# Four triangle layers on one core: centre and gate products as four 64x64 corners, whole squares in two layers, spread transposes ahead of the gate product

## The reference

```python
xn = _layernorm(x, ln1_w, ln1_b)                 # layers 0, 1, 2; layer 3 has none
left  = xn @ Wl.T * m * sigmoid(xn @ Wlg.T)      # mask m in layers 0, 1 and 3
right = xn @ Wr.T * m * sigmoid(xn @ Wrg.T)
out_gate = sigmoid(xn @ Wog.T)
out = einsum('bikd,bjkd->bijd', left, right)     # 64 planes of 192x192 products
out = _layernorm(out, ln2_w, ln2_b) * out_gate
return out @ Wout.T
```

## Time and profile before

| | before |
|---|---|
| median of 3 runs | 1425.36 us |
| the profiled execution's own time | 1427.8 us |
| its span, first to last instruction | 1425.6 us |
| TensorE matmul busy | 1231.4 us (86%) |
| VectorE busy | 983.5 us (69%) |
| ScalarE busy | 920.8 us (65%) |
| GpSimd busy | 525.5 us (37%) |
| mean granted TensorE clock | 0.972 |

### The profile page before, as it was taken

One profiled execution on the slowest core, in us unless ns is written; L12 is line 12 of the kernel. 1 busy time (PEld: TensorE's weight loads), 2 busy tenths in 40 slices (PEclk: granted clock), 3 DMA queues, 4 the chain that ended last, 5 costly groups with the idle time before them and its releaser, 6 DMA issues. The chain is left out here.

```text
span 1425.6 us, 39778 instructions
## 1 busy us (share of the span) xinstructions
PE 1231.4 (86%) x11486; PEld 686.5 (48%) x11486; DVE 983.5 (69%) x2692; ACT 920.8 (65%) x1849; POOL 525.5 (37%) x490
## 2 busy tenths in 40 slices
PE   0799998789799998999982999999888788899897
PEld 0455555434344544674331555567544344467443
DVE  6577776368779999226991888842299899931587
ACT  0577775399677777227992888842499677722676
POOL 0355553045355655003551666620155200000365
PEclk9999999999889999999995999999999999999999
DMA  8011111578623332797758555549799544469898
GB/s 296 23 51 50 50 50 64 140 230 263 202 90 105 105 110 84 211 297 217 204 158 326 156 170 176 185 142 298 251 288 282 183 156 155 149 186 313 263 315 267
DMA packets 222432, 258.73 MB, mean 181 GB/s; under 512 B 54177, under 2 KB 209057, under 8 KB 222369
## 3 DMA queue, kind: packets, MB, share of 16 engines
q1 hardware_dynamic: 193920, 232.75, 52.1%
q10 hardware_dynamic: 28448, 25.17, 5.4%
HBM read 139.89 MB, written 117.96 MB: 181 GB/s over the span
## 5 line engine op out<-in xcount | busy, mean ns | idle before, releaser
L1036 DVE SCALAR_TENSOR_TENSOR lr<-ps,mask,act_out 128x128 f32 (+5 forms) x1152 | 278.8, 310 | 51.1 <-ACT act_out L785 42.9
L1195 POOL TENSOR_TENSOR rstd<-ve,half_col 128x6 f32<-128x6 f32 x144 | 190.4, 1323 | 232.0 <-DVE ve L1003 196.5
L1240 POOL TENSOR_TENSOR new_ring<-val,lr 128x384 f32<-128x384 f32 x96 | 104.0, 1084 | 372.1 <-issue 297.8
L569 PE MATMUL ps<-w_parts,val 64*128 64x256 bf16 (+1 forms) x1728 | 199.7, 310 | 18.4 <-DVE lr L1036 17.7
L785 ACT ACTIVATE act_out<-ps 128x384 f32<-128x384 f32 x384 | 176.1, 483 | 50.5 <-PE ps L579 34.3
L1228 POOL TENSOR_TENSOR val<-act_out,gate_ring 128x384 f32<-128x384 f32 x96 | 99.8, 1040 | 224.8 <-ACT act_out L855 189.5
L679 PE MATMUL ps<-in_ring,k 128*128 128x384 f32 x288 | 124.4, 517 | 26.2 <-DMA in_ring<-t_scratch 23.0
L838 ACT ACTIVATE sq<-ps 128x384 f32<-128x384 f32 x192 | 105.7, 551 | 54.0 <-PE ps L679 52.0
L1087 DVE COPY cen<-ps 128x384 f32<-128x384 f32 x48 | 26.8, 558 | 159.1 <-PE ps L637 159.1
L637 PE MATMUL ps<-lr 64*128 64x192 f32 (+3 forms) x896 | 125.8, 331 | 9.8 <-DVE lr L1036 5.2
L761 ACT ACTIVATE cen<-ps,gn 128x384 f32<-128x384 f32 x144 | 83.8, 582 | 77.1 <-PE ps L524 73.8
(11 more groups left out here) (108 smaller groups left out, 2290.0 us busy)
## 6 DMA issues: line engine op xcount, KB each, us to landing
gate_scratch<-gate_ring SPq DMA_DIRECT2D x192, 192.0 KB, 2.2
gate_ring<-gate_scratch SPq DMA_DIRECT2D x96, 384.0 KB, 3.9
lr<-x_scratch SPq DMA_DIRECT2D x72, 384.0 KB, 4.9
in_ring<-t_scratch SPq DMA_DIRECT2D x72, 384.0 KB, 3.9
x_scratch<-new_ring SPq DMA_DIRECT2D x48, 384.0 KB, 3.4
in_ring<-x_scratch SPq DMA_DIRECT2D x96, 192.0 KB, 2.4
lr<-x SPq DMA_DIRECT2D x6, 1536.0 KB, 15.5
t_scratch<-cen SPq DMA_DIRECT2D x96, 96.0 KB, 4.0
```

The source lines that it names most:

```text
L569: mm = nc.tensor.matmul(banks[h][:, :, 0:P], moving(x, s)[half(h), N * r:N * r + P], proj_weights(w, h)[:, 0:2 * P], start=start, stop=sto ...
L1036: ins = nc.vector.scalar_tensor_tensor(out5[:, h, lo // 2:hi // 2, :, m], ps[:, 4 + 2 * r + h, lo:hi].rearrange("p (a e) -> p a e", e=2), ...
L1195: nc.gpsimd.tensor_tensor(rstd[:, s % 2, :], ve[:, s % 2, :], half_col[:, :], ALU.pow)\
```

## The change

The centre product and the gate product become four products of 64x64 corners of the block-diagonal weights each (`corners`), with 192 columns, which use the four quarters of the array. They swap the layout on the way: the partitions' half becomes the tile's row, and the bank (0 or 1) the picture's half; the gate product swaps it back. Both lie in banks 0 and 1, the centre in columns 0 to 191, the gate in 192 to 383, so that the centre product of tile n+4 now waits for the gate's sigmoid of tile n, and the gate product for `cen` of the tile in flight. Centre products have one place in place of two. The variance moves to bank 3. In layers 1 and 2 it is made of the whole float32 squares with `k_sel`, three products in place of six, and `square_low` is left out there. ScalarE squares `cen` out of SBUF in place of the PSUM result. TensorE's steps of these layers are written out with no loop.

```diff
+                def corners(first, weights, x, start, stop):
+                    for q in range(2):
+                        for e in range(2):
+                            mm = nc.tensor.matmul(ps[C * e:C * e + C, q, first:first + N], weights[half(q), half(q)],
+                                                  x[half(q), N * e:N * e + N], start=start, stop=stop,
+                                                  skip_group_check=True)
+                    return mm
...
-                    slot_free(pe, a_sq, base + n - 1)
-                    slot_free(pe, a_ve, base + n - 1)
-                    nc.tensor.matmul(ps[:, s % 2, 0:TILE], w_centre[:, :], in_ring[:, s, :] if l else x_all[:, n, :],
-                                     start=True, stop=True).then_inc(a_z, 1)
+                    slot_free(pe, a_cen, base + n)
+                    if gated:
+                        pe.wait_ge(a_gate, base + n - RING + 1)
+                    corners(0, w_centre, in_ring[:, s, :] if l else x_all[:, n, :], True, True).then_inc(a_z, 1)
...
+                    slot_free(pe, a_ve, base + n)
+                    if WHOLE_VAR[l]:
+                        pe.wait_ge(a_sq, base + n + 1)
+                        for j in range(CHUNKS):
+                            mm = nc.tensor.matmul(ps[:, 3, 2 * j:2 * j + 2], sq[:, s % 2, P * j:P * j + P], k_sel,
+                                                  start=True, stop=True)
...
+                    if ln:
+                        if centred:
+                            pe.wait_ge(a_cen, base + n + RING)
+                        for w, x in passes:
+                            mm = corners(N, gate_weights(w), moving(x, s), (w, x) == passes[0], (w, x) == passes[-1])
...
                 def step(n, i, s, ahead):
-                    gate(n, s)
                     if ln and ahead >= 1:
                         spread(n + 1, (s + 1) % RING)
+                    gate(n, s, ahead >= 3)
                     project(n, s, 0)
+                    if ln and ahead >= 4:
+                        centre(n + 4, i + 1, s, True)
                     project(n, s, 1)
-                    if ln and ahead >= 4:
-                        centre(n + 4, i + 1, s)
...
-                over_tiles(pe, step)
+                if ln:
+                    for n in range(TILES):
+                        step(n, n // RING, n % RING, TILES - 1 - n)
...
                     sigmoids(n, s, 0)
+                    if ln and ahead >= 4:
+                        centred(n + 4, s)
                     sigmoids(n, s, 1)
                     if ln and ahead >= 4:
-                        centred(n + 4, s)
+                        squared(n + 4, s)
...
-                    if ln and ahead >= 3:
+                    if halved and ahead >= 3:
                         square_low(n + 3, (s + 3) % RING)
```

More of the change, by code:

```diff
@@ L58 @@
 LATE = 14
+WHOLE_VAR = (False, True, True, False)
+LOWS = tuple(sum(1 for m in range(l) if not WHOLE_VAR[m]) for l in range(LAYERS))
 T_SCALE = (1.0, 1.0, 1.0 / N, 1.0)
@@ L514, in proj_weights, with centre @@
                     return w_parts[half(h), part, :] if IN_PARTS[l] else w_whole[half(h), :]
-                def centre(n, i, s):
+                def corners(first, weights, x, start, stop):
[5 more added lines that the diff above has]
+                    return mm
+                def centre(n, i, s, gated):
                     if l == 2:
@@ L542, in spread, with gate @@
                     mm.then_inc(a_bc, 1)
-                def gate(n, s):
+                def gate(n, s, centred):
                     if IN_PARTS[l]:
@@ L807, in phase_a @@
                 if ln:
-                    centred(0, 0)
-                    centred(1, 1)
-                    centred(2, 2)
-                    centred(3, 3)
+                    for n in range(RING):
+                        centred(n, n)
+                        squared(n, n)
                     high(0, 0)
@@ L989, in phase_a @@
                 ln = HAS_LN[l]
+                halved = ln and not WHOLE_VAR[l]
                 out5 = lr_view(l).rearrange("p a e (h r) -> p h a e r", h=2)
@@ L1032, in glu @@
                     if HAS_MASK[l]:
-                        for h in range(2):
+                        for g in range(2):
+                            h, row = (r, ROWS * n + g) if ln else (g, m)
                             for t, (lo, hi) in enumerate(((0, P), (P, COLS))):
                                 ins = nc.vector.scalar_tensor_tensor(
-                                    out5[:, h, lo // 2:hi // 2, :, m],
-                                    ps[:, 4 + 2 * r + h, lo:hi].rearrange("p (a e) -> p a e", e=2),
-                                    mask4[:, t, h, bass.ds(m, 1)],
-                                    sig[:, h, lo:hi].rearrange("p (a e) -> p a e", e=2), ALU.mult, ALU.mult)
+                                    out5[:, h, lo // 2:hi // 2, :, row],
+                                    ps[:, 4 + 2 * r + g, lo:hi].rearrange("p (a e) -> p a e", e=2),
+                                    mask4[:, t, h, bass.ds(row, 1)],
+                                    sig[:, g, lo:hi].rearrange("p (a e) -> p a e", e=2), ALU.mult, ALU.mult)
                         ins.then_inc(a_free, 1)
@@ L1066, in phase_a @@
                     normalise(0, 0)
+                if halved:
                     square_low(2, 2)
```

43 lines of the change are left out of this document (26 added, 17 removed).

## The result

The changed kernel takes 1447.08 us (median of 4 runs, 1440.95 to 1451.63) against 1424.13 for the kernel before on the same chip: ratio 1.0155, 95% interval 1.0109 to 1.0202. It is slower by 1.6%; the forecast was 1424 with a range to 1438. The profiled execution took 1447.88, its span is 1445.6, TensorE's mean granted clock 0.967.

A forecast was written before the change was run, and what follows sets the result against it. TensorE was taken to bound layer 0 narrowly, VectorE's ring layer 1, TensorE with waits for `low` layer 2. Terms +3.5, 0, -4.2 and -1 (phase starts) sum to -1.7 us, giving 1424 us, range 1410 to 1438.

The forecast's parts named there:

- TensorE bounds it, but by little: Layer 0 before the change: TensorE's work sets the tile, 3.91 us, 3.95 with loop turns.
- the second ring: Layer 0's cycle of projection, sigmoid, `glu`, projection, put at 3.72 us, only 0.23 shorter than TensorE's work.
- the sum of 3.67: Layer 0: the pieces of the projection, sigmoid and `glu` cycle without the centre product, added up and checked against measured 3.72.
- Layer 0's 4.03: Forecast tile time in layer 0 with the centre product inside the cycle, against 3.95 before: +3.5 us over 44 tiles.
- The unrolled loop gives nothing: its 0.15 a turn lies in TensorE's new wait: Layer 0: writing out TensorE's loop saves no time, since the 0.15 us a turn falls where TensorE waits anyway.
- Layer 1, 0 us,: VectorE's ring stays at 3.64 us a tile, with ScalarE's second sigmoid fitting by 0.05; bounds -2 and +5.
- Layer 2, 3.30 a tile and -4.2 us,: Layer 2's tile falls from 3.395 to 3.30 us, -4.2 us over 44 tiles; bounds -11.5 and +9.
- The wait of the centre for the gate's sigmoid: Layer 2: `centre(n+4)` waits about 0.11 us a tile for the gate's sigmoid of n, bringing 3.13 to 3.24.
- TensorE's own work: Layer 2: TensorE's work without waits, 3.15 + 0.52 variance - 0.39 centre - 0.15 gate, is 3.13 us a tile.
- Some 0.06 for what is left of L1202 and `low` meeting: Layer 2: a chosen 0.06 us a tile for GpSimd's L1202 and VectorE's `low` still delaying each other.
- The slower rival: Layers 1 and 2: whole-square passes cost more than 0.11 us, deciding from about 0.13; total 1438 to 1446, chance 0.15.
- The clock: Layer 0: TensorE's waits might lower its granted clock, making the tile 5 us and the kernel 50 slower; chance 0.02.

The follow-up runs named there:

- e1: Changed kernel with the centre product and ScalarE's `cen` moved back behind the second projection and sigmoid: 1434.94 us, ratio 1.0046 to the kernel before.
- e4: Kernel before with only TensorE's loop over the tiles written out in layers 0 to 2: 1435.89 us, ratio 1.0048.
- e8: Kernel before with only VectorE's loop over the tiles written out in layers 0 and 1: 1419.90 us, ratio 0.9954.
- e13: Changed kernel with only VectorE's loop written out in layers 0 and 1: 1434.22 us, ratio 1.0043 to the kernel before.
- e7: Changed kernel with e1's and e5's edits and VectorE's loop written out in layers 0 and 1: 1413.71 us, ratio 0.9918 to the kernel before.
- e5: Changed kernel with SyncE's `keep` store issued ahead of the gathers in layer 2: 1445.74 us, ratio 1.0119 to the kernel before.
- e11: Kernel before with only the spread transposes of tile n+1 moved ahead of the gate product of n: 1419.32 us, ratio 0.9960.
- e3: e5 with the gate product of n again ahead of the spread transposes of n+1: 1437.72 us, ratio 1.0076 to the kernel before.

## Why the prediction was wrong

- **"TensorE bounds it, but by little" and the second ring** held in kind. TensorE idles for `glu` as forecast, and the centre in the ring costs 0.33, forecast 0.36. That the sum of 3.67 met the measured 3.72 was partly luck. The earlier trace rows lie in the last four tiles, which are written out behind the loop; `glu` starts 0.53 behind the first sigmoid there, while the sum's 0.65 is the loop's (0.65 in the step of the earlier trace rows too). ScalarE's and VectorE's timelines of the kernel before beside the earlier trace rows:

```profile
239.47 0.49 ACT L785 ACTIVATE act_out<-ps 128x384 f32<-128x384 f32 x1 [0.28 <-PE ps L579]
```

```profile
240.00 1.89 DVE L1036 SCALAR_TENSOR_TENSOR lr<-ps,mask,act_out 128x128 bf16<-128x128 f32 x8 [1.36 <-ACT act_out L785]
```

  In the loop the ring without the centre is 3.85 (e1), 0.06 under TensorE's 3.91 and not some 0.2.
- **Layer 0's 4.03** was mis-sized, in one term: "four of the eight `glu` 0.90, back to TensorE 0.14", 1.04 in all, measured 1.13 (0.90, and 0.23 back). Sigmoid to `glu` was 0.67, forecast 0.65. 4.11 in place of 4.03, and 4.13 with the turns.
- **"The unrolled loop gives nothing: its 0.15 a turn lies in TensorE's new wait"** failed. The turn in layer 0 is in good part VectorE's: it stayed in e4 and went in e8 and e13. Once VectorE stood in the ring that binds, its loop cost 6.9 us there (192.9 to 186.0), and 9.3 between e1 and e7.
- **Layer 1, 0 us,** held; the window lost 1.7, mostly at its start, and ScalarE's slack of 0.05 was enough.
- **Layer 2, 3.30 a tile and -4.2 us,** is the step that turned the sign: measured 3.60 a tile and +8.1 us. (a) The loop written out was costed at nothing, and nothing was said of SyncE. Its chain of 6.65 stood in the trace beside TensorE's 6.79. By itself the loop costs +9.2 (e4), in the changed kernel 4.8 (e5). (b) The wait of the centre for the gate's sigmoid was named and halved: 0.11, measured 0.22. ScalarE starts 0.50 behind the gate product's start (forecast 0.46), and the centre 0.72 behind the sigmoid's start (forecast 0.63). (c) TensorE's own work was 3.23, not 3.13: variance 0.69 for 0.67, gate 0.38 for 0.35, the narrow groups around the centre 0.50 for 0.47, the spread 0.45 for the 0.42 of the tile that took 3.15.
- **"Some 0.06 for what is left of L1202 and `low` meeting":** `low` took 0.56 in all but two of 47 tiles; GpSimd's L1243 took 0.83 to 1.17, no more than L1202 before (0.83 to 1.23), and nothing waited for it.
- **The slower rival**, whole-square passes above 0.11 each, was near: 0.69 for six is 0.115, under its point of 0.13. The sign came out as in that rival, by other mechanisms. *The clock* did not fall in layer 0's waits.
- **The two rules weighed.** The Trainium skill, TensorEngine Tiling (Array Packing), section Key Properties, says that a change of tiling mode drains TensorE. TensorE's own work exceeded the sum by 0.10 with one such change more a tile, but the rows do not separate a drain from the small differences of four groups, so that it cost anything here is not shown. The experiments keep the waits on shared banks for the reason that the Trainium skill, PSUM — Partial Sum Buffer, section PSUM bank collisions raise a hardware error, gives: accesses of two engines to one bank and the same partitions must not overlap. No run here shows what would happen otherwise.
- **Left open:** which of two equally long chains binds e7's layer 0, and about 5 us of medians outside the tiles in kernels with whole squares.

## What to carry to other kernels

List the chains that close over a DMA queue (issue, landing, next issue) with their period, beside the rings of the compute engines: one with 0.1 us of slack in 6.8 shows in no wait of a compute engine until something stretches it. A loop written out, or left a loop, is a change of its own: on TensorE it cost 9 us by its traffic, on VectorE leaving it one cost 5 to 9 in a layer whose ring it stood in. And check a sum against rows of the same part of a loop: the last tiles, behind it, ran by another price. When two products are put into the same banks, each waits for the eviction of the other; a move in the program that gains with banks apart (e11, -0.4%) may cost with banks shared (e3 against e5).

## What was unexpected of the hardware

A single gather issue on SyncE took up to 1.44 us in place of 0.60 when it started within 0.65 behind an instruction transfer on q8 (all 14 long ones of the changed kernel), and the ten `keep` stores of e4 with a q8 transfer near their issue landed after 3.55 to 4.71 us, the twelve others after 2.51 to 3.09. VectorE's first `glu` started 0.53 behind the sigmoid's start with VectorE's loop written out and 0.67 in the loop, with the same instructions. With VectorE's loop written out q8's packets stayed at 36 (e8), with TensorE's they rose to 76 (e4): what q8 carries more in these kernels is TensorE's. And a layer may begin at the lower level of TensorE's clock for some 10 us more in one execution than in another: e5's layer 1 was at 0.50 from 400 to 412 us and 0.68 in the next 12, the changed kernel at 0.70 and 1.00, which is 5 us a layer, as much as several of the effects studied here.
